# Edge scoring of a graph attention layer: VectorE operands of two tiles or chunks at a time, and another split of the PSUM banks

## The reference, cut to what matters

```python
hr_src = h_r[:, src]
hr_dst = h_r[:, dst]
diff = hr_dst - hr_src
score = s_src + s_dst + einsum(diff, a_dif) + einsum(abs(diff), a_abs) + einsum(hr_src * hr_dst, a_prd)
alpha = leaky_relu(score, 0.2)
```

## Time and profile before

| | us |
|---|---|
| median of 3 timed runs (1384.03 to 1385.01) | 1384.72 |
| span of the profiled execution, first to last instruction | 1491.0 |
| scoring in that execution, first `hot` to last product | 214 to 765 |
| busy in the whole span: PE / DVE / ACT / POOL | 1294.3 / 1103.9 / 735.2 / 757.0 |
| share of busy time in the span: PE / DVE / ACT / POOL | 87% / 74% / 49% / 51% |
| mean granted TensorE clock, as a share of full | 0.925 |

### The profile page before, as it was taken

One profiled execution on the slowest core, in us unless ns is written; L12 is line 12 of the kernel. 1 busy time (PEld: TensorE's weight loads), 2 busy tenths in 40 slices (PEclk: granted clock), 3 DMA queues, 4 the chain that ended last, 5 costly groups with the idle time before them and its releaser, 6 DMA issues. The chain is left out here.

```text
span 1491.0 us, 23856 instructions
## 1 busy us (share of the span) xinstructions
PE 1294.3 (87%) x6804; PEld 828.0 (56%) x6805; DVE 1103.9 (74%) x2258; ACT 735.2 (49%) x1237; POOL 757.0 (51%) x858
## 2 busy tenths in 40 slices
PE   6999967989999999999967788888888856999986
PEld 2555534545555555555536566766776733777763
DVE  8998876999999999999989576766676776122116
ACT  5555415878888888888851000000000272555541
POOL 1201035666666666666536655655655501455551
PEclk9999978999999999999987889988989965999998
DMA  9233357888888889888847877766766237344478
GB/s 241 89 114 140 128 185 247 278 252 261 291 268 277 278 273 287 268 280 276 260 101 221 274 270 245 243 212 218 242 205 209 79 129 244 115 134 131 136 249 305
DMA packets 141701, 322.60 MB, mean 216 GB/s; under 512 B 30163, under 2 KB 46279, under 8 KB 141595
## 3 DMA queue, kind: packets, MB, share of 16 engines
q0 software_dynamic: 62816, 212.87, 45.5%
q1 hardware_dynamic: 74524, 103.15, 20.5%
q10 hardware_dynamic: 4256, 5.24, 1.0%
HBM read 255.27 MB, written 65.93 MB: 215 GB/s over the span
## 5 line engine op out<-in xcount | busy, mean ns | idle before, releaser
L1309 PE MATMUL m_ps<-msg,hot 128*128 128x260 f32 x1344 | 337.1, 410 | 56.4 <-issue 51.4
L1309 PEld LDWEIGHTS m_ps<-msg,hot 128*128 128x128 f32 x1344 | 273.6, 205 | 120.0 <-issue 74.8
L1146 POOL DMA_INDIRECT rows<-he_d,target x234 | 231.2, 988 | 139.8 <-DVE msg L1227 73.9
L929 PE MATMUL gs_ps<-room,hot_t 128*128 x1008 | 278.0, 386 | 6.6 <-DVE hot_t L783 3.7
L1005 ACT ACTIVATE rows<-rows,raw_a 128x512 f32<-128x512 f32 x336 | 273.6, 814 | 11.2
L1003 ACT ACTIVATE rows<-d_ps 128x512 f32<-128x512 f32 x336 | 196.0, 583 | 99.7 <-PE d_ps L942 52.8
L794 DVE TENSOR_TENSOR rows<-rows 128x512 f32<-128x512 f32 x336 | 229.6, 683 | 9.7 <-ACT rows L1005 4.9
L1227 DVE TENSOR_TENSOR msg<-rows,room 128x512 f32<-128x512 f32 x336 | 211.9, 683 | 0.8
L765 POOL DMA_INDIRECT x_sb<-table_d,target x150 | 150.1, 1001 | 96.8 <-PE d_ps L942 65.7
L1163 ACT COPY room<-m_ps 128x520 f32<-128x520 f32 x20 | 11.8, 592 | 370.6 <-PE m_ps L1309 220.2
L929 PEld LDWEIGHTS gs_ps<-room,hot_t 128*128 128x128 bf16 x1008 | 92.5, 99 | 122.1 <-issue 79.9
(11 more groups left out here) (342 smaller groups left out, 1787.6 us busy)
## 6 DMA issues: line engine op xcount, KB each, us to landing
rows<-early_d SPq DMA_DIRECT2D x84, 256.0 KB
early_d<-x_sb SPq DMA_DIRECT2D x51, 256.0 KB
x_sb<-local_d SPq DMA_DIRECT2D x84, 128.0 KB
early_d<-rows SPq DMA_DIRECT2D x33, 256.0 KB
table_d<-rows POOLq DMA_DIRECT2D x10, 520.0 KB, 3.3
both_d<-rows POOLq DMA_DIRECT2D x10, 520.0 KB, 4.3
he_d<-he SPq DMA_DIRECT2D x20, 256.0 KB, 2.0
both_d<-he SPq DMA_DIRECT2D x20, 256.0 KB, 2.3
```

The costliest lines, as they stand in the source:

```text
L929: pe.matmul(gs_ps[:, use(n, t) % 3, :], h, hrs[:, bass.ds(blk, 1), piece, :].rearrange("p a f -> p (a f)"), start=(piece == 0), stop=(piec ...
L1146: pool.indirect_dma_start(g[:, r, t, :, :, :].rearrange("p c h d -> p (c h d)"), None, he_d, bass.IndirectOffsetOnAxis(ap=k["target"][:, q ...
L1309: last = pe.matmul(m_ps[:, bass.ds(slot[t], 1), j, 0:HEADS // 2 * HW].rearrange("p a f -> p (a f)"), hot[:, r, t, :], halves[:, r, t, j, : ...
```

## The change

`gs_ps` gets four banks, used as two pairs; a pair holds the source rows of two tiles. `lin_ps` goes from two banks to one. `subtract` takes two tiles at once (128 x 1024), after both have been fetched; `times` takes two chunks at once. `fetch` raises `gathered` with the third of its large matmuls, and the four small matmuls of the linear terms move behind the fourth fetch of the strip (`linear_terms`), with a wait for the sum of the strip before. TensorE's order is otherwise the same, `reduce(n-2)` still stands between `turn(n-1,2)` and `fetch(n,3)`, and its first matmul waits for both product pairs. VectorE's turn becomes

```diff
--- before.py
+++ after.py
@@ -684,6 +684,7 @@
 
 
     PICK_AT, LEAD_AT = 2, 2 + TG + 1
+    PAIRS = GT // 2
     hrs, lins, att = k["hrs"], k["lins"], k["att"]
     raw, heads, cin = k["raw_a"], k["heads"], k["cin"]
     with ExitStack() as ctx:
@@ -709,15 +710,16 @@
         fpart = s.sb("fpart", [P, TG])
         ends = s.sb("ends", [P, 4])
         carry = s.sb("carry", [P, 2])
-        gs_ps = s.ps("gs_ps", [P, 3, F])
+        gs_ps = s.ps("gs_ps", [P, 4, F])
         d_ps = s.ps("d_ps", [P, 2, LC])
         sc_ps = s.ps("sc_ps", [P, LC])
-        lin_ps = s.ps("lin_ps", [P, 2, F])
-        lin_row = lin_ps[:, 0, :]
+        lin_bank = s.ps("lin_ps", [P, F])
+        lin_ps = lin_bank[:, 0:GT * 3 * HEADS]
+        lin_row = lin_bank[:, :]
 
         picked = sem("runs_picked")
         got, locs = k["rows_in"], k["locals_in"]
-        lin_summed = sem("lin_summed")
+        lin_made, lin_summed = sem("lin_made"), sem("lin_summed")
         hots, gathered, dready, dturned = sem("hot_ready"), sem("src_rows"), sem("diff_ready"), sem("diff_turned")
         abr, ur, vr, red, extras = sem("abs_ready"), sem("u_ready"), sem("v_ready"), sem("reduced"), sem("extras_ready")
         kept = sem("strip_kept")
@@ -726,7 +728,8 @@
         shift_done, exped, att_turned, att_kept = sem("max_subtracted"), sem("exped"), sem("att_turned"), sem("att_kept")
         k.update(att_turned=att_turned, att_kept=att_kept)
         order = ORDER
-        use = lambda n, t: GT * n + t + min(max(n - PICK_AT + 1, 0), TG + 1)
+        use = lambda n, pair: PAIRS * n + pair + min(max(n - PICK_AT + 1, 0), TG + 1)
+        home_pair = lambda i: gs_ps[:, 2 * (i % 2):2 * (i % 2) + 2, :]
 
         def on_sync(sp):
             def keep_early(n):
@@ -780,24 +783,30 @@
             mark = k["dve_chain"].mark
             def one_hot(n):
                 dve.wait_ge(locs[n % LRING], 16 * (n // LRING + 1))
+                if n >= 2:
+                    dve.wait_ge(lin_made, n - 1)
                 dve.tensor_scalar(hot[:, n % 2, :], spread[:, n % LRING, :], k["line"][:, :], None, ALU.is_equal).then_inc(hots, 1)
 
-            def subtract(n, t):
-                if t == 0:
+            def subtract(n, pair):
+                if pair == 0:
                     dve.wait_ge(got[n % RING], 16 * GT * (n // RING + 1))
-                dve.wait_ge(gathered, GT * n + t + 1)
-                row = rows_of(n)[:, t, 0:F]
-                dve.tensor_tensor(row, row, gs_ps[:, use(n, t) % 3, :], ALU.subtract).then_inc(dready, 1)
-
-            def times(n, c):
-                dve.wait_ge(ur, CH * n + c + 1)
-                dve.tensor_tensor(uv[:, n % 2, c, :], uv[:, n % 2, c, :], ab[:, n % 2, c, :], ALU.mult).then_inc(vr, 1)
+                dve.wait_ge(gathered, GT * n + 2 * pair + 2)
+                rows = rows_of(n)[:, 2 * pair:2 * pair + 2, 0:F]
+                dve.tensor_tensor(rows, rows, home_pair(use(n, pair)), ALU.subtract).then_inc(dready, 1)
+
+            def times(n, pair):
+                both = slice(2 * pair, 2 * pair + 2)
+                dve.wait_ge(ur, CH * n + 2 * pair + 2)
+                dve.tensor_tensor(uv[:, n % 2, both, :], uv[:, n % 2, both, :], ab[:, n % 2, both, :], ALU.mult).then_inc(vr, 1)
 
             def add_lin(n):
                 tg, st = order[n]
                 if tg >= 2 and st == 0:
                     dve.wait_ge(red, STRIPS * (tg - 1))
-                dve.tensor_reduce(lin_sum[:, :, :], lin_ps[:, n % 2, 0:GT * 3 * HEADS].rearrange("p (t i h) -> p t h i", t=GT, i=3),
+                dve.wait_ge(lin_made, n + 1)
+                if n >= 1:
+                    dve.wait_ge(extras, n)
+                dve.tensor_reduce(lin_sum[:, :, :], lin_ps.rearrange("p (t i h) -> p t h i", t=GT, i=3),
                                   AX_X, ALU.add).then_inc(lin_summed, 1)
                 dve.wait_ge(lin_summed, n + 1)
                 dve.tensor_tensor(extra[:, tg % 2, :, :, st, :], lin_sum[:, :, :].rearrange("p t (c h) -> p t c h", c=CH),
@@ -807,7 +816,7 @@
                 n = t + PICK_AT
                 width = LC if t < TG else 1
                 dve.wait_ge(picked, t + 1)
-                dve.tensor_scalar(pen[:, t * LC:t * LC + width], gs_ps[:, (use(n, 0) - 1) % 3, 0:width], -1.0, BIG,
+                dve.tensor_scalar(pen[:, t * LC:t * LC + width], home_pair(use(n, 0) - 1)[:, 0, 0:width], -1.0, BIG,
                                   ALU.add, ALU.mult).then_inc(dready, 1)
 
             def lead_penalties(tg):
@@ -846,22 +855,14 @@
                 if n < G:
                     subtract(n, 0)
                 if inside(n - 2):
-                    times(n - 2, 3)
+                    times(n - 2, 1)
+                if n + 1 < G:
+                    one_hot(n + 1)
                 if n < G:
                     subtract(n, 1)
-                if n + 1 < G:
-                    one_hot(n + 1)
+                    add_lin(n)
                 if inside(n - 1):
                     times(n - 1, 0)
-                if n < G:
-                    subtract(n, 2)
-                if inside(n - 1):
-                    times(n - 1, 1)
-                if n < G:
-                    subtract(n, 3)
-                    add_lin(n)
-                if inside(n - 1):
-                    times(n - 1, 2)
                 if 0 <= n - LEAD_AT < TG:
                     lead_penalties(n - LEAD_AT)
                 for step in range(4):
@@ -906,9 +907,9 @@
             def pick(t):
                 n = t + PICK_AT
                 i = use(n, 0) - 1
-                pe.wait_ge(dready, i - 2)
+                pe.wait_ge(dready, i - 1)
                 width = LC if t < TG else 1
-                pe.matmul(gs_ps[:, i % 3, 0:width], k["pick"][:, t, :, :, :].rearrange("p c s h -> p (c s h)"),
+                pe.matmul(home_pair(i)[:, 0, 0:width], k["pick"][:, t, :, :, :].rearrange("p c s h -> p (c s h)"),
                           k["runs"][:, 0:width], start=True, stop=True).then_inc(picked, 1)
 
             def blocks_of(n):
@@ -922,20 +923,26 @@
             def fetch(n, t, blk):
 
                 pe.wait_ge(hots, n + 1)
-                if use(n, t) >= 3:
-                    pe.wait_ge(dready, use(n, t) - 2)
+                i = use(n, t // 2)
+                if t % 2 == 0 and i >= 2:
+                    pe.wait_ge(dready, i - 1)
                 h = hot[:, n % 2, t * P:(t + 1) * P]
                 for piece in range(3):
-                    pe.matmul(gs_ps[:, use(n, t) % 3, :], h, hrs[:, bass.ds(blk, 1), piece, :].rearrange("p a f -> p (a f)"),
-                              start=(piece == 0), stop=(piece == 2))
-                if t == 0 and n >= 2:
-                    pe.wait_ge(extras, n - 1)
-                pe.matmul(lin_ps[:, n % 2, t * 3 * HEADS:(t + 1) * 3 * HEADS], h,
-                          lins[:, bass.ds(blk, 1), :, :].rearrange("p a i f -> p (a i f)"),
-                          start=True, stop=True).then_inc(gathered, 1)
+                    last = pe.matmul(home_pair(i)[:, t % 2, :], h, hrs[:, bass.ds(blk, 1), piece, :].rearrange("p a f -> p (a f)"),
+                                     start=(piece == 0), stop=(piece == 2))
+                last.then_inc(gathered, 1)
+
+            def linear_terms(n, blocks):
+
+                if n >= 1:
+                    pe.wait_ge(lin_summed, n)
+                for t, blk in enumerate(blocks):
+                    last = pe.matmul(lin_ps[:, t * 3 * HEADS:(t + 1) * 3 * HEADS], hot[:, n % 2, t * P:(t + 1) * P],
+                                     lins[:, bass.ds(blk, 1), :, :].rearrange("p a i f -> p (a i f)"), start=True, stop=True)
+                last.then_inc(lin_made, 1)
 
             def turn(n, c):
-                pe.wait_ge(dready, use(n, GT - 1) + 1)
+                pe.wait_ge(dready, use(n, PAIRS - 1) + 1)
                 if CH * n + c >= 2:
                     pe.wait_ge(abr, CH * n + c - 1)
                 for t in range(GT):
@@ -956,8 +963,8 @@
                                   extra[:, tg % 2, t, :, :, :].rearrange("p c s h -> p (c s h)"), k["ident"][:, :],
                                   start=False, stop=False, skip_group_check=True)
                 for c in range(CH):
-                    if n == G - 1 or c == 0:
-                        pe.wait_ge(vr, CH * n + (c + 1 if n == G - 1 else CH))
+                    if c == 0:
+                        pe.wait_ge(vr, PAIRS * n + PAIRS)
                     last = pe.matmul(sc_ps[32 * c:32 * (c + 1), :], heads[:, column], uv[:, n % 2, c, :],
                                      start=(st == 0), stop=final, tile_position=(0, 32 * c), skip_group_check=True)
                 last.then_inc(red, 1)
@@ -970,6 +977,8 @@
                 for t in range(GT):
                     if n < G:
                         fetch(n, t, blocks[t])
+                        if t == GT - 1:
+                            linear_terms(n, blocks)
                     if 1 <= n <= G:
                         turn(n - 1, t)
```

## The result

The changed kernel takes 1504.21 us (1502.98 to 1507.05 in four runs) against 1384.87 us for the kernel before: a ratio of 1.0856, with a 95% interval of 1.0837 to 1.0876. It is 119 us slower; the prediction was 1483 us, +98. The profiled execution of the changed kernel has a span of 1501.8 us and took 1503.56 us, so it is a usual one. For the trace of before on which the prediction rests this does not hold, and the first experiment comes back to it.

What follows compares the result with a forecast made beforehand. VectorE and TensorE, both nearly full at 6.30 us a strip, would bind in a closed loop of 6.97 + 0.35 = 7.32 us. Loop +82, end +1, clock +15 make +98: 1384.72 + 98 = 1483 us, range 1452 to 1525.

Steps and rivals of the forecast that it cites:

- The closed loop: Scoring stage: TensorE and VectorE wait for each other from one reduction to the next, 6.97 us a strip without group work.
- A merged operation: VectorE's 128x1024 subtractions and products: 1.145 us each in place of 2 x 0.60, saving 0.22 us a strip.
- The linear terms: Four small matmuls in a row on TensorE: 0.4 us in place of 4 x 0.03, at no cost overall.
- The group work: VectorE's lead scans, penalties and group scores: inside the loop with nothing to hide them, +0.35 us a strip.
- The clock: TensorE's clock falls to half after longer idle times in strips with group work: 8 falls of about 2 us, +15 us.
- Rival A: TensorE in scoring: ordinary strips' 1.0 us idle also trips the clock, some 35 falls, 1538 us; chance 0.12.
- The mis-sized term: Scoring in the kernel before: a strip takes 6.30 us, against 7.32 after, so 80 x 1.02 = +82 us.
- TensorE's late signals: Fetch signals to VectorE, 0.86 us instead of 0.21: if only from profiling, the loss is 106 us rather than 82.
- ScalarE, GpSimd and the DMA queues: Scoring stage: ScalarE, 5.4 of 7.3 us a strip, is outside the loop; the others get more time a strip.

Runs made afterwards that it cites:

- experiment 1: The kernel before, unchanged, traced once more: 1387.59 us.
- Experiment 3: The changed kernel with times(n-2,1) ahead of subtract(n,0) on VectorE: 1409.6 us, ratio 1.0176 to before.
- experiment 4: The changed kernel with reduce(n-2) moved to the end of TensorE's turn, behind fetch(n,3) and turn(n-1,3): 1374.16 us, ratio 0.9918 to before.
- experiment 2: The changed kernel with each merged subtraction and product given as two 128x512 operations, order and waits kept: 1525.94 us, ratio 1.1024 to before.
- experiment 7: The changed kernel with lead_penalties and strip_scores moved between one_hot(n+1) and subtract(n,1) on VectorE: 1471.68 us, ratio 1.0623 to before.

## Why the prediction was right, step by step

- *The closed loop* was forecast at 6.97 us and is 6.96, term by term as listed above. Experiment 3 takes one subtraction out of it, and strips without group work fall from 6.95 to 5.89, by nearly that operation's 1.15; experiment 4 opens it, and they fall to 5.58; experiment 2 lengthens its four operations, and they rise to 7.19. So this is shown. What the prediction did not do is to sum the same path for the kernel before, about 4.8 us by experiment 1. Its reason, that the product stands behind a subtraction with two fetches instead of one, is not what made it longer, since that subtraction does not wait (438.64). The path has the same operations as before, and each of the four large ones handles two tiles or chunks where it handled one.
- *A merged operation* was put at 1.145 us of VectorE and 1.226 in full; the trace has 1.14 to 1.15 and 1.222. In experiment 2 its absence costs 22 us against the 18 of 80 x 0.22.
- *The linear terms* were put at 0.4 us and take 0.10; they are not in the loop, so the sum did not feel it. I had priced them by the pitch of the transpositions, which was the wrong row.
- *The group work* stood in the loop as forecast: moving it into the gap gave back 32.5 us with the clock falls, against 25 + 10 in that run's expectation. The penalties cost more than the 0.6 us that I gave them: six early strips of the changed kernel take 7.75 to 7.79, which is 0.8 over 6.95. In the trace the penalty at 246.20 is followed by the subtraction at 247.01, 0.81 us later and 0.92 after the start of its fetch. TensorE had idled 0.72 us before the first fetch of that pair (245.00), released by a subtraction (L795): the penalty uses a pair of banks, so this fetch has to wait for the other. That would explain the 0.2 us over 0.6; no run tests it.
- *The clock* was put at 8 falls of 2 us. There are 7. Strips with the same work take 9.15 us with a fall near and 7.65 without (third step of a group's scores), and the strip beside it is 8.3 and not 8.2: about 1.6 us for each of four falls; the six strips with a lead scan, with the other three, sum to 52.8 us where 6 x 8.25 = 49.5 were due. Together some 10 us, not 15. The row behind the term, is from the disturbed execution, and experiment 1 has no fall in that stage; that the number of falls came out near 8 is luck. The warning of the Trainium skill, "TensorE: Matmul & The Clock Gate", "Why this matters for your kernels", speaks only of longer gaps and would have had no falls; this trace has seven after idle times of 2.24 to 2.34 us. Rival A, that ordinary strips trip the clock too, falls: experiment 7 has 1.0 us of idle time in each strip and no fall after the first ones.
- *The mis-sized term* is the time of a strip before, 6.30 us "from 400 / 63.5". It is 6.00 in a usual execution (mean over 79 strips of experiment 1). That is 80 x 0.30 = 24 us, and 98 + 24 = 122; less the 5 that the clock was put too high, 117, against 119 measured. The prediction saw the cause, TensorE's late signals, named them as a reason for "1.3 x 80 = 106 rather than 82", and took the smaller number. What it had was a span 106 us over the median and no account of where they were; the fit between 5.54 us of VectorE's work, 0.35 of group work and 0.1 of waiting would have been the better guess.
- *ScalarE, GpSimd and the DMA queues* were left out of the sum. In the trace after, VectorE waits 6.9 us for gathers in the first strips (before 232) and 2.3 us for ScalarE at the end (from 843), and never for them between.

## What to carry to other kernels

When the order of work on two engines is written by hand, follow the chain from one wait back to itself, across both engines, before counting what an instruction saves: here handing over two tiles at a time saves 0.22 us of VectorE's time a strip, but it doubles each of the four operations that stand between one reduction and the next, 4.8 to 6.96 us, and that cost 1.45 us a strip. Before, at 4.8 us, the path lay below the 5.5 to 5.6 us that each of the two engines had to do for a strip, and cost little; so sum it before and after the change. If all engines show idle time and two name each other as releasers, look for such a loop and cut it by moving one item in one queue; then put small work into what gaps remain, in pieces that fit. And if the span of a trace differs from the timed median, by 7.7% here, take a second trace before the first is used for sums.

## What was not expected of the hardware

In the first trace of before VectorE waited 37 times for a fetch in the scoring, and 31 of these signals reached it 0.56 to 1.14 us after the small matmul's start, in place of 0.21, while the instructions lasted as long as ever. The same kernel on another execution had none of it and was 105 us shorter in span (1385.8 against 1491.0), 37 us of that in the scoring. What disturbed it is not shown. In the scoring of the changed kernel the clock fell for 3.41 us at a time around the end of idle times of TensorE of 2.24 to 2.34 us, though not of every one, and not for idle times of 1.0 us repeated in all strips. In experiment 2 three of ten falls came after 1.90 us.
